# Remainders of q and k taken by GpSimd from a copy that ScalarE makes, in a single-core attention kernel on Trainium2

## The reference, cut to what matters

```python
def _L0_attn_ref(x, Wq, Wk, Wv, Wo):
    H = 16; HD = 16; WINDOW = 128; N_GLOBAL = 1
    q = (x @ Wq.T).reshape(Bb, Tt, H, HD).transpose(0, 2, 1, 3)   # k and v alike
    attend = (abs(i - j) <= WINDOW) | (i < N_GLOBAL) | (j < N_GLOBAL)
    logits = jnp.einsum('bhqd,bhkd->bhqk', q, k) * SCALE
    logits = jnp.where(attend[None, None, :, :], logits, -jnp.inf)
    weights = jax.nn.softmax(logits, axis=-1)
    out = jnp.einsum('bhqk,bhkd->bhqd', weights, v)
    return out.transpose(0, 2, 1, 3).reshape(Bb, Tt, Dd) @ Wo.T
x = x + _L0_attn_ref(_layernorm(x, axis=-1), Wq, Wk, Wv, Wo)
```

## Time and profile before

| | before |
|---|---|
| median of 3 runs | 870.6 us (869.64 to 871.29) |
| span of the profiled execution | 867.2 us |
| median less that span | 3.4 us |
| TensorE matmul busy | 814.6 us, 94% |
| VectorE busy | 758.3 us, 87% |
| ScalarE busy | 637.2 us, 73% |
| GpSimd busy | 488.1 us, 56% |
| mean granted TensorE clock | 0.997 |

### The profile page before, as it was taken

The page is one execution under the profiler, slowest core; times in us unless marked ns, Lnnn a source line. Parts: engine busy times, 40 slices in busy tenths (PEclk is TensorE's granted clock), DMA queues, the critical chain, the costliest instruction groups (busy, mean ns, idle before and its releaser), DMA issues. The chain is left out here.

```text
span 867.2 us, 50607 instructions
## 1 busy us (share of the span) xinstructions
PE 814.6 (94%) x21504; PEld 606.9 (70%) x21505; DVE 758.3 (87%) x2819; ACT 637.2 (73%) x1417; POOL 488.1 (56%) x874
## 2 busy tenths in 40 slices
PE   9798999999999999999999999898999999999894
PEld 8555667767777777667778777666778777766572
DVE  7898899989887899998987899998988889998785
ACT  2268888897877667998877666898777766888850
POOL 3212556675555557765554465675554556656763
PEclk9999999999999999999999999999999999999998
DMA  7722224432212344441213335352222335220113
GB/s 231 116 81 75 67 73 121 135 88 70 77 62 96 111 146 119 120 127 62 89 51 101 106 105 161 108 131 71 74 73 68 106 93 149 94 77 18 49 51 102
DMA packets 93191, 83.51 MB, mean 96 GB/s; under 512 B 17568, under 2 KB 92192, under 8 KB 92960
## 3 DMA queue, kind: packets, MB, share of 16 engines
q1 hardware_dynamic: 91360, 78.91, 30.1%
q10 hardware_dynamic: 1600, 1.31, 1.0%
HBM read 20.66 MB, written 8.39 MB: 33 GB/s over the span
## 5 line engine op out<-in xcount | busy, mean ns | idle before, releaser
L1105 ACT ACTIVATE probs<-bank 128x384 f32<-128x384 f32 (+1 forms) x1024 | 462.8, 480 | 146.8 <-PE bank L962 137.4
L1431 DVE CUSTOM_DVE_ANT_0 bank<-bank,con 128x288 f32<-128x288 f32 x1024 | 494.4, 518 | 53.2 <-PE bank L934 44.8
L934 PE MATMUL bank<-k_stack,q_stack 96*32 96x288 bf16 x4096 | 325.4, 288 | 10.7 <-DVE row_max L1431 5.7
L962 PE MATMUL bank<-q_stack,k_stack 99*32 99x288 bf16 (+2 forms) x4096 | 319.8, 285 | 16.0 <-ACT probs L1105 9.7
L980 PE MATMUL bank<-probs,v_sb 128*32 128x128 f32 x5888 | 305.4, 272 | 3.6 <-issue 1.5
L1218 POOL TENSOR_SCALAR_AFFINE_SELECT probs<-probs 128x512 f32<-128x512 f32 x240 | 154.8, 645 | 180.1 <-ACT probs L1105 179.5
L980 PEld LDWEIGHTS bank<-probs,v_sb 128*32 128x32 f32 x5888 | 192.1, 110 | 36.7 <-issue 5.3
L962 PEld LDWEIGHTS bank<-q_stack,k_stack 99*32 99x32 bf16 x4096 | 123.6, 95 | 79.7 <-ACT probs L1105 53.5
L934 PEld LDWEIGHTS bank<-k_stack,q_stack 96*32 96x32 bf16 x4096 | 127.3, 95 | 74.0 <-DVE row_max L1431 21.3
L1223 POOL TENSOR_SCALAR_AFFINE_SELECT probs<-probs 128x512 f32<-128x512 f32 x240 | 154.1, 642 | 19.3 <-ACT probs L1105 19.2
L823 PE MATMUL bank<-xnT,wqk_sb 128*32 128x256 f32 x2048 | 158.1, 379 | 0.6 <-DVE neg_max L1453 0.5
(11 more groups left out here) (126 smaller groups left out, 737.2 us busy)
## 6 DMA issues: line engine op xcount, KB each, us to landing
q_stack<-pieces SPq DMA_DIRECT2D x384, 64.0 KB, 2.7
k_stack<-pieces SPq DMA_DIRECT2D x364, 64.0 KB, 2.7
x_ring<-in_x SPq DMA_DIRECT2D x28, 512.0 KB, 4.5
out_x<-x_ring SPq DMA_DIRECT2D x16, 512.0 KB, 3.9
attn<-in_x SPq DMA_DIRECT2D x4, 512.0 KB, 6.0
wback_sb<-in_wback SPq DMA_DIRECT2D x8, 256.0 KB, 6.0
k_stack<-pieces ACTq DMA_DIRECT2D x20, 64.0 KB, 3.6
q_stack<-neg_max SPq DMA_DIRECT2D x48, 16.0 KB, 2.3
```

The lines of the kernel that those rows point to most:

```text
L934: last = pe.matmul(a_ring[i % len(a_ring)][SP * s:SP * (s + 1), 0:WIN], q_stack[g % 2][0:KROWS, h, q:q + SP], k_stack[g % 2][0:KROWS, h, q ...
L962: last = pe.matmul(b_ring[i % len(b_ring)][SP * s:SP * (s + 1), start:final], k_stack[g % 2][0:SROWS, h, WINDOW + P * j + SP * s:WINDOW + ...
L1105: act.activation(probs[:, j % 4, h, c0:c1], b_ring[i % len(b_ring)][:, c0:c1], ACT.Exp, scale=LOGIT_SCALE).then_inc(S["exp_ready"], 1)
L1431: dve.tensor_tensor_reduce(out=a_ring[i % len(a_ring)][:, 0:WIN], in0=a_ring[i % len(a_ring)][:, 0:WIN], in1=mask, scale=1.0, scalar=con[: ...
```

## The change

For groups 1 to 15 the event REST is replaced by two. `QK_COPY`, on ScalarE right behind PIECE1, copies the QK bank to `rest` in float32 and frees the bank. `REST_LEFT`, on GpSimd one quarter later, subtracts the first piece from `rest` in place. PIECE2 now waits for that, and moves from two quarters behind `done` to four, PIECE3 from two to five. Group 0 stays as it was.

```diff
+        REST_AT = {'REST': 1, 'PIECE2': 4, 'PIECE3': 5}
@@ stages
                     opening(done, "PIECE1", n, c)
-                    end(done, "REST", n, c)
-                    opening(done + 2, "PIECE2", n, c)
-                    end(done + 2, "PIECE3", n, c)
+                    if n:
+                        opening(done, "QK_COPY", n, c)
+                        end(done + REST_AT["REST"], "REST_LEFT", n, c)
+                        opening(done + REST_AT["PIECE2"], "PIECE2", n, c)
+                        end(done + REST_AT["PIECE3"], "PIECE3", n, c)
+                    else:
+                        end(done, "REST", n, c)
+                        opening(done + 2, "PIECE2", n, c)
+                        end(done + 2, "PIECE3", n, c)
@@ schedule
-        EMPTIED = {..., "REST": "QK", "PIECES": "TURN_MAX",
+        EMPTIED = {..., "REST": "QK", "QK_COPY": "QK", "PIECES": "TURN_MAX",
@@ ScalarE
+                        elif kind == "QK_COPY":
+                            g, c = n
+                            act.wait_ge(S["piece3_ready"], 4 * g + c)
+                            act.activation(rest[:, :], bank_of("QK", g, c)[:, :], ACT.Copy)\
+                               .then_inc(free_sem("QK", g, c), 1)
                         elif kind == "PIECE2":
-                            act.wait_ge(*emptied("QK", g, c))
+                            if g:
+                                act.wait_ge(S["rest_ready"], i - 3)
+                            else:
+                                act.wait_ge(*emptied("QK", g, c))
@@ GpSimd
+                        elif kind == "REST_LEFT":
+                            g, c = n
+                            i = 4 * g + c
+                            pool.wait_ge(*emptied("QK", g, c))
+                            pool.wait_ge(S["piece1_ready"], i + 1)
+                            pool.tensor_tensor(rest[:, :], rest[:, :], pieces[i % 2][:, 0, :],
+                                               ALU.subtract).then_inc(S["rest_ready"], 1)
```

More of the change, by code:

```diff
@@ L140, in build @@
                  "row_copied", "row_recip", "row_ready", "first_row", "s0_ready",
-                 "piece1_ready", "piece2_ready", "piece3_ready", "stack0", "stack1", "stack2", "stack3",
+                 "piece1_ready", "piece2_ready", "piece3_ready", "rest_ready", "stack0", "stack1", "stack2", "stack3",
                  "a_full", "a_free", "key0_ready", "max_piece", "max_rest", "max_stacked", "p0_diff",
@@ L517, in build @@
         PARTED = ("PROJECT", "QK", "VALUES", "FIRST")
-        EMPTIED = {"XT_IN": "XT", "TURN_ATTN_IN": "TURN_ATTN", "PROJECT_IN": "PROJECT", "REST": "QK", "PIECES": "TURN_MAX",
+        EMPTIED = {"XT_IN": "XT", "TURN_ATTN_IN": "TURN_ATTN", "PROJECT_IN": "PROJECT", "REST": "QK", "QK_COPY": "QK", "PIECES": "TURN_MAX",
                    "OUT_MULT": "TURN", "VALUES_IN": "VALUES", "FIRST_IN": "FIRST", "FOLD_IN": "FOLD"}
```

## The result

The changed kernel takes **892.15 us** (median of 4 runs, 889.48 to 893.11) against 870.12 us for the kernel before, run beside it (median of 4, 868.48 to 871.29). The ratio is 1.0239, with a 95% interval of 1.0208 to 1.0270: some 21 us slower. The forecast was slower by 7.2 us with a range to 886: the direction was right, the size was a third of what came.

A forecast was written before the change was run, and what follows sets the result against it. No engine alone bounds the kernel, but ScalarE ends TensorE's waits most often. Terms -1.2 + 6.0 - 1.2 + 0 + 2.4 - 3.6 + 2.9 + 1.9 = +7.2 us on 870.6 gave 877.8 us, range 866 to 886.

The forecast's parts named there:

- about 15: 15 of the 60 REST_LEFT come right behind an RSTD chain; ScalarE's PIECE2 waits there about 0.5 us each.
- Three signs: Group 0 shorter by 1 us; groups 7 and 11 longer by over 1; VectorE's busy time down about 41, less overlap.
- +6.0, 0, +2.4 and +2.9: Copy, us: groups 1, 2, 3, 7, 11 +6.0; 4, 8, 12 0; 5, 9, 13 +2.4; 6, 10, 14 +2.9.
- the ring hides most: Groups 5, 9, 13: two PSUM banks hide most of each copy; 0.2 x 12 = +2.4 us.
- Halving the copy in groups 6, 10 and 14: VectorE nearly full there; half of 12 x 0.49 us counted for the copy, +2.9.
- -1.2 -1.2 -3.6: VectorE's relief, us: group 0 -1.2; groups 1, 2, 3, 7, 11 -1.2; groups 6, 10, 14 -3.6.
- a quarter of 7.5 us: PIECE2 behind a late GpSimd, mostly groups 6, 10, 14: 15 x 0.5 = 7.5 us, a quarter counted, +1.9.
- Rival A: GpSimd becomes the gate: all 7.5 us counts, 20 copies cost 0.49 each, CUTs late; 887.2 us, chance 0.20.
- Rival B: VectorE is the bound in groups 0, 6, 10, 14: faster, 865.6 us, at best 861.6; chance 0.20.
- Rival C: Relief and copy meet the same waits and cancel: 870.6 us, within 1.7 us; chance 0.10.
- The moves at nothing: PIECE2 and PIECE3 move by two and three quarters; 3 us of cover are left for STACK's DMAs; costed at nothing.
- The estimate of 1.35 us: GpSimd's subtraction at 1.96 times VectorE's time; if it held, 0.7 us in all. The forecast took 1.16 us.

The follow-up runs named there:

- the doubled copy: Kernel before, with two spare bf16 ScalarE copies directly behind each PIECE1 of groups 1 to 15: 914.9 us, ratio 1.0506.
- m2_copy: Kernel before, with one spare float32 ScalarE copy directly behind each PIECE1 of groups 1 to 15: 888.97 us against 872.57, ratio 1.0189.
- m3_relief: Kernel before, with VectorE's subtraction cut to one of 512 columns for groups 1 to 15: 868.3 us against 872.57, ratio 0.9949.
- m4_thin: Changed kernel, with GpSimd's subtraction cut to one of 512 columns: 886.15 us, ratio 1.0162.
- m13_mended: Changed kernel, PIECE2 six and PIECE3 seven quarters behind the QK, save chunk 1 of each batch's second group: 880.70, 881.12, 889.88 us, ratio 1.0167.
- m5_vector: Changed kernel, with REST_LEFT done by VectorE instead of GpSimd: 887.56 us, ratio 1.0170.
- m1_moved: Kernel before, with only PIECE2 and PIECE3 moved to four and five quarters for groups 1 to 15: 872.85 us against 872.57, ratio 1.0008.
- m8_three: The change for chunks 0 to 2 of group 1 alone, all others as before: 869.1 us against 871.05, ratio 0.9982.
- m9_apart: Kernel before, with the spare ScalarE copy one quarter behind PIECE1: 886.73 us, ratio 1.0182.
- m11_far: Kernel before, with the spare ScalarE copy eight quarters behind PIECE1: 876.34 us, ratio 1.0081.
- m7_later: Changed kernel, with PIECE2 six quarters behind the QK instead of four and PIECE3 seven instead of five: 889.5 us, ratio 1.0211.
- m10_spread: Changed kernel, copy one quarter later, GpSimd's subtraction two quarters behind the QK, PIECE2 six and PIECE3 seven: 885.87 us, ratio 1.0160.

## Why the prediction was right in direction and wrong in size

- **The mechanism** was right in its parts: ScalarE ends TensorE's waits, the copy lengthens them, relief of VectorE buys little, PIECE2 stands for GpSimd behind RSTD. Durations, the rise of the exp waits and the fall of the maxima's waits came as said; 21 waits of PIECE2 against "about 15". Three signs failed: group 0 is not shorter (38.83 against 37.18 us, or as long once the clock is taken into account), group 11 is 0.1 us shorter and not over 1 us longer, and VectorE's busy time fell by 23 us only. The forecast lacks 13.6 of the 20.8 us: 5.1 in the copy, 1.6 in the relief, 4.8 in GpSimd, and 2.1 that are put down to nothing.
- **The term that failed first is the copy.** The sum had +6.0, 0, +2.4 and +2.9 = 11.3 us; alone it measured 16.4. By groups its profile gives 7.1, 0.2, 5.1 and 4.4. The wrong step is "the ring hides most" of groups 5, 9 and 13, taken at 0.2 us a copy: it was 0.4. TensorE never resting did not mean that ScalarE had room: behind a PIECE1 of these groups ScalarE was already 93% busy over four quarters, and the doubled copy shows that what is added on top counts nearly in full. Halving the copy in groups 6, 10 and 14 was the second slip: in m2_copy they grew 1.6, 0.8 and 2.0 us, 4.4 together against 2.9.
- **The relief** had -1.2 -1.2 -3.6 = -6.0; alone it measured -4.4. "Half of it" for the groups that are 96% busy was too much: in m3_relief's profile groups 6 and 10 gave 0.5 and 0.8 us and group 14 got 0.7 longer, 0.6 together against 3.6. VectorE's fullness was not what set those groups' pace. Group 0's 1.2 us is not seen either. That the whole was off by 1.6 only is in part luck: the gain stood in other groups than the sum had it.
- **GpSimd** had +1.9, a quarter of 7.5 us; it measured 6.7 (thin) and 6.3 (mended). Both factors were too small. PIECE2 stood 21 times and 13.9 us, 0.66 us each, against 15 times 0.5; and about half of that reached the time, not a quarter. I let group 6's 12.9 us of ScalarE idle pay for a stall at another time. That is the same mistake as with the copy.
- **Rival A** named 887.2 us and is nearer than my sum; I gave it 0.20 and cut the range inside it, at 886. It had GpSimd's full price. Its other half, 0.49 us for each of the 20 copies of groups 1, 2, 3, 7 and 11, stood in the wrong place: these cost 0.35 each, and what was missing lay in groups 5, 6, 9, 10, 13 and 14. Its late CUTs were not seen.
- **Rival B** needed the copies and the late PIECE2 to cost under 5 us; they cost 16.4 and 6.7. Its price, 0.60 us for each of 15 subtractions and 9.0 in all, is more than the 4.4 us (2.8 to 6.0) of m3_relief; its half of 5 us would fit, but not in the groups that it named. **Rival C** falls with all runs of the copy.
- **The moves at nothing** held (1.0008), and no cost of GpSimd's load shows once PIECE2 is late enough.
- The estimate of 1.35 us from the Trainium skill (GPSIMD Engine Reference, Performance versus the Vector engine) did not hold here: the subtraction took 1163 ns, 1.69 times VectorE's 688, as PIECE3's row said, and 1.67 times the 698 ns of VectorE's own subtraction from `rest` in m5_vector.

## What to carry to other kernels

Where two engines hand banks to each other in a short ring, don't pay for a new instruction with the other engine's or its own idle time summed over a stretch: find out whether the engine idles *within the next few instructions*. Here a copy that occupies ScalarE for 0.49 us cost 0.12 us where ScalarE was 73% busy over the next four quarters, 0.27 where it was 94% busy, and a second one there 0.46, with the share of the whole span at 73% to 76% in every case. And an instruction moved to a third engine can cost by when it ends, though its load costs nothing that shows: look at what stands before it in that engine's order.

## What was not expected of the hardware

In the opening TensorE's granted clock fell in some executions. Of the changed kernel, from 26 and from 28 us, ahead of the first changed instruction (length, busy PE, PEld, DVE, ACT, POOL, then the clock):

```profile
26.00:28.00 2.00, 1.21 (x24) 0.84 (x28) 1.65 (x6) 0.00 (x0) 0.00 (x0) 0.90 0.98 167
28.00:30.00 2.00, 2.00 (x22) 0.87 (x18) 0.90 (x5) 0.00 (x0) 0.00 (x0) 0.50 1.06 128
```

The clock is at 0.50, 1.2 of 2.4 GHz, after TensorE was busy 0.66 of the 2 us from 24 us, waiting for the first stacks' DMAs. The first step, from its first mask to the next step's, then took 3.66 us instead of 2.22. In the profiled execution of before TensorE idled through those 2 us and the clock stayed at 1.00, as it did from 28 to 30 us in 9 of the 14 profiled kernels; 5 had the dip, m1_moved and m3_relief among them. So the dip isn't the change's, and it explains most of group 0's 1.7 us in the changed profile. Even if every execution of the changed kernel had it and none of before, it would be 1.4 of the 21 us.

It also bears on single groups. Of the other nine profiles only those of before and m4_thin are free of such a dip in their middle: m2_copy, m8_three, m9_apart, m11_far and m13_mended have 0.57 from 39 to 43 us, and m7_later, m10_spread and m13_mended 0.72 from 140 to 146 us, in group 2. Why a dip comes in one execution and not in the other was not settled.
